# A gated cross-attention and expert layer on one core: loads, casts and the first routing scores are put in another order

## The reference

```
x = x + tanh(g_xattn) * GAT2(GAT1(ctx, adj=layernorm(x)))     # leaky relu, softmax with mask 1e10*(1-adj), elu
n = layernorm(x)
logits = tanh(n @ Wg1.T) @ Wg2.T                              # 8 experts
scores = softmax of the top 2 logits, 0 elsewhere
h = silu(n @ Wup[e].T + bup[e])
x = x + tanh(g_ffn) * sum_e scores[:, e] * (h @ Wdown[e].T + bdown[e])
```

## Time and profile before

| | us |
|---|---|
| median of 3 runs | 97.99 |
| the three runs | 96.74, 97.99, 98.16 |
| the profiled execution's own time | 96.72 |
| its span, first to last instruction | 94.9 |
| between span and time | 1.8 |

### The profile page before, as it was taken

How to read it: one execution, slowest core, us unless ns; L and a number is a source line. 1 busy time by engine, 2 the same in 40 slices (tenths; PEclk the granted TensorE clock), 3 DMA queues, 4 the chain that set the end, 5 groups by cost and what they waited for, 6 DMA issues and landing times.

```text
span 94.9 us, 1971 instructions
## 1 busy us (share of the span) xinstructions
PE 84.5 (89%) x621; PEld 78.9 (83%) x621; DVE 66.9 (70%) x206; ACT 53.4 (56%) x128; POOL 44.4 (47%) x100
## 2 busy tenths in 40 slices
PE   5959999969989689999999999999999999999800
PEld 5936878659878578998999899999999999999700
DVE  5844968374689929999879738977438767889520
ACT  0519785489692761439790979855536555443100
POOL 7910869829018422999780000787100888810000
PEclk9999999999999999999999999999999999999997
DMA  1999990000000000000000000030000030003022
GB/s 26 296 294 410 418 327 6 0 0 0 7 3 0 0 0 0 0 7 3 0 0 3 0 7 0 0 110 3 7 0 0 0 110 0 0 0 116 5 68 67
DMA packets 3339, 5.44 MB, mean 57 GB/s; under 512 B 474, under 2 KB 2684, under 8 KB 3068
## 3 DMA queue, kind: packets, MB, share of 16 engines
q1 hardware_dynamic: 2952, 4.74, 15.0%
q10 hardware_dynamic: 372, 0.53, 1.8%
HBM read 4.21 MB, written 1.05 MB: 55 GB/s over the span
## 4 chain that ended last, share of the span: by engine, by line
PE 52%; DVE 27%; issue 5%; DMA 5%; ACT 4%; POOL 1%; DVEq 1%; ACTq 1%
PE bank L850 6%; PE bank L714 5%; PE bank L759 5%; DMA w_sb<-in_w 5%; PE bank L715 5%; PE bank L719 5%; PE bank L761 5%; PE bank L760 5%; DVE hid_lo L1064 4%; PE bank L874 4%; DVE stat L966 3%; PE bank L734 3%; DVE wdown_hi L1199 2%; DVE xa L1148 2%; DVE hid L1056 2%
## 5 line engine op out<-in xcount | busy, mean ns | idle before, releaser
L504 ACT ACTIVATE act_sb<-bank,small_sb 128x256 f32<-128x256 f32 x32 | 15.1, 472 | 13.7 <-PE bank L719 13.6
L1056 DVE TENSOR_TENSOR hid<-act_sb,bank 128x256 f32<-128x256 f32 x32 | 13.3, 418 | 10.4 <-PE bank L734 8.5
L512 ACT CAST hid_hi<-hid 128x256 fp32r<-128x256 f32 x32 | 13.0, 407 | 11.1 <-DVE hid L1056 10.4
L759 PE MATMUL bank<-wdown_hi,hid_hi 128*128 128x256 f32 x64 | 18.3, 287 | 0.3 <-ACT hid_hi L512 0.3
L714 PE MATMUL bank<-xt_hi,wup_hi 128*128 128x256 f32 x64 | 18.0, 303 | 0.4 <-DVE xa L1148 0.3
L761 PE MATMUL bank<-wdown_hi,hid_lo 128*128 128x256 f32 x64 | 18.0, 281 | 0.0
L760 PE MATMUL bank<-wdown_lo,hid_hi 128*128 128x256 f32 x64 | 18.0, 281 | 0.0
L715 PE MATMUL bank<-xt_hi,wup_lo 128*128 128x256 f32 x64 | 16.5, 280 | 0.0
L1064 DVE TENSOR_TENSOR hid_lo<-hid,hid_hi 128x256 fp32r<-128x256 f32 x32 | 13.5, 422 | 0.3
L714 PEld LDWEIGHTS bank<-xt_hi,wup_hi 128*128 128x128 f32 x64 | 12.1, 189 | 1.0 <-DVE xa L1148 0.5
L719 PE MATMUL bank<-xt_lo,wup_hi 128*128 128x256 f32 x64 | 12.8, 281 | 0.0
(11 more groups left out here) (145 smaller groups left out, 183.5 us busy)
## 6 DMA issues: line engine op xcount, KB each, us to landing
x_sb<-in_x SPq DMA_DIRECT2D x4, 256.0 KB, 4.8
wup_sb<-in_wup SPq DMA_DIRECT2D x1, 1024.0 KB, 7.4
wdown_sb<-in_wdown SPq DMA_DIRECT2D x1, 1024.0 KB, 9.6
out<-out_sb SPq DMA_DIRECT2D x3, 256.0 KB, 2.2
check_sb<-in_check_w SPq DMA_DIRECT2D x1, 320.0 KB
w_sb<-in_w ACTq DMA_DIRECT2D x1, 256.0 KB, 5.0
out<-out_sb SPq DMA_DIRECT2D x2, 128.0 KB, 2.8
ctx_sb<-in_ctx_t ACTq DMA_DIRECT2D x1, 128.0 KB, 4.1
```

The source lines that it names most:

```text
L504: nc.scalar.activation(act_out(n), bank[:, UP[n % 2], 0:N], ACT.Silu, bias=bup_sb[:, k % E:k % E + 1]).then_inc(silu_rdy, 1)
L512: nc.scalar.copy(hid_hi[:, n % HID_SLOTS, :], hid[:, n % 2, :]).then_inc(hid_hi_rdy, 1)
L759: nc.tensor.matmul(dst, hid_hi[:, n % HID_SLOTS, part], wdown_hi[:, e, :], start=False, stop=False, skip_group_check=True)
L1056: nc.vector.tensor_tensor(hid[:, n % 2, :], act_out(n), bank[:, PICK[n % 2], 0:N], ALU.mult).then_inc(hid_rdy, 1)
```

## The change

- Loads. `w0` comes first on SP's queue, then `x` of graph 0, `w1`, `x` of graph 1, the bias row, and the rest as before. ACT's queue carries only the context, now in two pieces: graph 0 and then graphs 1 to 3.
- PE is given 10 products on the constant tile instead of 16. `feat0(2)` stands ahead of `turn(0)`, `feat1(0, 1)` ahead of `twice_part(0)`, and `turn(3)` and `twice_part(3)` move from the loop to the first part. `gather(1)` writes to bank 1 instead of bank 5, so `pe_up` of step 1 waits for `gated(0)` alone, and `pe_pick` of step 0 waits for `gated(1)`. `gather(3)` comes at step 4 instead of 5, the first scores' transpose at step 3 instead of 5.
- DVE. `dve_route` stands right behind `dve_logits`, in seven chained steps instead of nine; `elu1(3)`, `gated(1)` and its statistics come after it. `turned(2)` comes ahead of `dve_norm`, `turned(3)` behind `dve_xt`. `gated` of graphs 1 to 3 is one instruction on 512 elements instead of two on 256. DVE makes `veps` and `nmean` (two small instructions for each graph), which POOL made.
- ACT takes the four `wdown` casts (steps 1, 3, 5, 7), copies `source` of graph 3 at step 0 instead of 4, casts the bias row behind `exp0(0)` instead of first of all, and casts the second quarter of `wup` earlier.
- POOL takes the cast of `pick` (before its one-hots) and both instructions on `bdown`, and makes the one-hots of graph 3 after the first `wup` quarter.

The gathers themselves are the same instructions as before.

PE, the last rows ahead of the loop and its first steps, before. In these listings `x2` and the like count equal instructions in a row.

The diff, cut to its core:

```diff
-WARM_MMS = 16
+WARM_MMS = 10
-SCORE_PLACE = (5, 6, 6, 6)
+SCORE_PLACE = (3, 6, 6, 6)
-        TURN, TWICE, FEAT0, FEAT1, GATHER = (2, 2, 2, 7), (0, 0, 6, 7), (6, 7, 4, 6), (1, 3, 1, 3), ((4, 5), (5, 5), (6, 6), (7, 7))
+        TURN, TWICE, FEAT0, FEAT1, GATHER = (2, 2, 2, 7), (0, 0, 6, 7), (6, 7, 4, 6), (1, 3, 1, 3), ((4, 5), (1, 1), (6, 6), (7, 7))
 # SP
+            sp.dma_start(w0_sb[:], w0).then_inc(w0_ld, 16)
             load_x(0)
+            sp.dma_start(w1_sb[:], w1).then_inc(w1_ld, 16)
             load_x(1)
-            sp.dma_start(ctx_sb[0:FIN, 2 * N:T], ctx_t[:, 2 * N:T]).then_inc(ctx2_ld, 16)
+            sp.wait_ge(bias_zero, 1)
+            sp.dma_start(bias_sb[0:33:32, :], bias_2).then_inc(bias_ld, 16)
 # row_power, POOL
-            pool.wait_ge(mv_rdy, (nb + 1) * C)
-            nc.gpsimd.tensor_scalar(veps[:, pair(b)], mv[:, pair(b), 1], EPS, None, ALU.add).then_inc(veps_rdy, 1)
-            nc.gpsimd.tensor_scalar(nmean[:, pair(b)], mv[:, pair(b), 0], -1.0, None, ALU.mult).then_inc(veps_rdy, 1)
 # POOL
+            pool.wait_ge(pick_raw, 2)
+            nc.gpsimd.tensor_copy(pick[:], pick_f).then_inc(pick_rdy, 1)
+            rows_onehot(1)
+            rows_onehot(2)
             wup_part(0)
             row_power(pool, 0, 0)
+            rows_onehot(3)
             wup_part(1)
             wup_part(2)
+            row_power(pool, 0, 1)
             wup_part(3)
             wdown_part(0)
+            wdown_part(1)
             row_power(pool, 0, 2)
+            nc.gpsimd.tensor_copy(bdown_parts[:], bdown_sb[:]).then_inc(bdown_hi_rdy, 1)
...
 # ACT
-            act.dma_start(ctx_sb[0:FIN, 0:2 * N], ctx_t[:, 0:2 * N]).then_inc(ctx_ld, 16)
-            act.dma_start(w0_sb[:], w0).then_inc(w0_ld, 16)
-            act.dma_start(bias_sb[0:33:32, :], bias_2).then_inc(bias_ld, 16)
-            act.dma_start(w1_sb[:], w1).then_inc(w1_ld, 16)
+            act.dma_start(ctx_sb[0:FIN, 0:N], ctx_t[:, 0:N]).then_inc(ctx_ld, 16)
+            act.dma_start(ctx_sb[0:FIN, N:T], ctx_t[:, N:T]).then_inc(ctx2_ld, 16)
             minus0(0)
             exp0(0)
+            bias_part()
-            act_experts(act, 0, {4: [lambda: source_copy(3)]})
+            act_experts(act, 0, {0: [lambda: source_copy(3)], 1: [lambda: wdown_part(0)],
+                                 3: [lambda: wdown_part(1)], 5: [lambda: wdown_part(2)], 7: [lambda: wdown_part(3)]})
 # PE, pe_up and pe_pick
-                pe.wait_ge(xa_rdy, C * (n + 1))
+                pe.wait_ge(xa_rdy, n + 1)
-            if n < 2:
-                pe.wait_ge(z_rdy, n + 3)
+            if n == 0:
+                pe.wait_ge(xa_rdy, 2 * C)
+            if n == 1:
+                pe.wait_ge(z_rdy, B)
-            pe_experts(pe, 0, {1: [lambda: gather(2), lambda: turn(3)], 3: [lambda: twice_part(3)], 5: [lambda: gather(3)]})
+            pe_experts(pe, 0, {1: [lambda: gather(2)], 4: [lambda: gather(3)]})
 # DVE
             gated(0)
-            stats(0)
+            dve_stats(dve, 0, 0)
+            turned(2)
             dve_norm(dve, 0)
-            turned(2)
...
             dve_logits(dve, 0, 0)
-            gated(1)
-            stats(1)
-            nc.vector.tensor_copy(bdown_parts[:], bdown_sb[:]).then_inc(bdown_hi_rdy, 1)
             dve_route(dve, 0)
             elu1(3)
+            gated(1)
+            dve_stats(dve, 0, 1)
-            dve_experts(dve, 0, {0: [lambda: wdown_part(0)], 1: [lambda: turned(3), lambda: gated(2)],
-                                 2: [lambda: wdown_part(1), lambda: stats(2)], 3: [pick_copy], 4: [bdown_part, lambda: wdown_part(2)],
-                                 6: [lambda: gated(3), lambda: wdown_part(3)], 7: [lambda: stats(3)], 13: [check_peaks],
+            dve_experts(dve, 0, {0: [lambda: gated(2), lambda: dve_stats(dve, 0, 2)],
+                                 5: [lambda: gated(3), lambda: dve_stats(dve, 0, 3)], 13: [check_peaks],
```

More of the change, by code:

```diff
@@ L146, in build @@
         hit = sb("hit", [P, 2, NT, E])
+        same, hit0, prob0 = sb("same", [P, C, 2, E]), sb("hit0", [P, C, 2, E]), sb("prob0", [P, C, 2])
         score = sb("score", [P, NT, E])
@@ L557, in source_copy @@
                 act.wait_ge(twice_mm, b + 1)
-                nc.scalar.copy(source_next[:, b - 1, :, :], both(TWICE[b])).then_inc(source_nextdy, 1)
+                nc.scalar.copy(source_next[:, b - 1, :, :], both(TWICE[b])).then_inc(source_rdy, 1)
             def minus0(b):
@@ L589, in _ @@
             exp1(0)
+            turned(1)
             minus0(3)
             exp0(3)
-            turned(1)
             act.wait_ge(small_ld, 16)
@@ L595, in _ @@
             wup_part(0)
+            wup_part(1)
             source_copy(1)
@@ L599, in _ @@
             exp1(1)
-            wup_part(1)
+            source_copy(2)
             act_xt(act, 0, 0)
@@ L604, in _ @@
             exp1(2)
-            source_copy(2)
             act_gate(act, 0, 0)
@@ L884, in _ @@
             feat0(1)
+            feat0(2)
             turn(0)
-            feat0(2)
             feat1(0, 0)
+            feat1(0, 1)
             twice_part(0)
-            feat1(0, 1)
             feat0(3)
@@ L900, in _ @@
             feat1(2, 1)
+            turn(3)
             feat1(3, 0)
@@ L969, in dve_stats @@
                 nc.vector.bn_aggr(mv[:, t, :], stat[:, t, :]).then_inc(mv_rdy, 1)
+            dve.wait_ge(mv_rdy, C * (run * B + b + 1))
+            nc.vector.tensor_scalar(veps[:, pair(b)], mv[:, pair(b), 1], EPS, None, ALU.add).then_inc(veps_rdy, 1)
+            nc.vector.tensor_scalar(nmean[:, pair(b)], mv[:, pair(b), 0], -1.0, None, ALU.mult).then_inc(veps_rdy, 1)
         def dve_norm(dve, run):
@@ L1145, in gated @@
                     dve.wait_ge(gates_rdy, 1)
+                if b > 0:
+                    dve.wait_ge(gather_mm, C + b)
+                    nc.vector.scalar_tensor_tensor(out=xa[:, pair(b), :], in0=both(GATHER[b][0]), scalar=gates[:, 0:1],
+                                                   in1=x_sb[:, pair(b), :], op0=ALU.mult, op1=ALU.add).then_inc(xa_rdy, C)
+                    return
                 for t in range(C):
-                    dve.wait_ge(gather_mm, t + 1 if b == 0 else C + b)
+                    dve.wait_ge(gather_mm, t + 1)
                     nc.vector.scalar_tensor_tensor(out=xa[:, C * b + t, :], in0=bank[:, GATHER[b][t], t * D:(t + 1) * D],
@@ L1180, in _ @@
             dve_xt(dve, 0, 0)
+            turned(3)
             elu1(2)
```

77 lines of the change are left out of this document (37 added, 40 removed).

## The result

The changed kernel takes **93.27 us** (median of 4 runs, 92.65 to 93.88), the kernel before in the same set of runs 98.07 us (96.74 to 98.78). The ratio is 0.9553 with a 95% interval of 0.943 to 0.9677. The forecast was 93.4 us. The profiled execution took 93.16 us, of which 91.4 us are span; the sum for such an execution was 93.2 us.

The account below looks back on a forecast made before the run. PE bounds from 43 us; from 26.2 to 43 DVE is fuller, earlier engines wait in a chain. 96.72 - 3.3 (three parts) - 0.2 = 93.2, plus 0.2: 93.4 us; own range 92.5 to 94.0, 8 in 10: 92.3 to 95.3.

Parts of the forecast that it names:

- part 1: Head: new load order brings data 2.1 us earlier, graph 0's statistics 0.8 us earlier; bounds -0.1 and -1.3.
- part 2: Norm of graph 0: `veps` and `nmean` on DVE save 0.4 us, `turned(2)` ahead of the power's wait 0.45.
- transposes to step 0: PE works without a gap, 5.8 us plus 0.7 moved from the loop; step 0 starts at 25.3 us.
- rival A: Head gives nothing: data at 4.9 us, bias row late or pace low; 94.0 us, chance 0.20.
- Part 3: Steps 0 to 7: 4.7 us leave DVE, PE's waits of 2.0 us go; 13.0 us become 10.6.
- term of -0.2: Behind step 8: one PE wait, for a silu late under DVE's backlog, goes; -0.2 us.
- rival B: DVE's `veps` and `nmean` of graphs 2 and 3 wait out POOL's `wdown_lo`, delaying `hid`: +1.6, 94.8 us, chance 0.12.
- C: ACT bounds steps 0 to 7, casts standing ahead of silus: full price 2.4 us, 95.6 us, chance 0.08.
- D: Slower than before: PE stays at 1.2 GHz well into the first part; up to 100.7 us, chance 0.04.
- E: New load order holds up graph 1's `x` or `wup`: +1 to 2 us, 94.4 to 95.4, chance 0.04.
- 0.2 us for the spread: Added to the sum because work begins at 4.0 us, so a late rise of PE's pace costs at least as much.
- rule on shared interfaces: GpSimd and VectorE share SBUF interfaces, so more POOL work means more DVE collisions; counted against the change, no separate size.

Follow-up runs that it names:

- old loads: Changed kernel with the old load order and queues, 16 constant products and early bias cast: 94.44 us, ratio 0.9724.
- order alone: Changed kernel's PE, ACT, DVE and POOL order, shorter scores' chain and one-instruction `gated`, with loads, norm and casts of the kernel before: 98.87 us, six runs in two groups.
- repetition: Changed kernel run again, nothing altered but a blank line: 93.32 us, ratio 0.9625.
- old norm: Changed kernel with `veps` and `nmean` on POOL for all graphs and `turned(2)` behind the wait for the power: 94.45 us, ratio 0.9773.
- old casts: Changed kernel with the `wdown`, `pick` and `bdown` casts back on DVE, in the new order: 96.12 us, ratio 0.984.
- casts alone: Kernel before with only the `wdown` casts moved to ACT and `pick` and `bdown` to POOL: 97.22 us, ratio 1.0035.
- `nmean` on POOL: Changed kernel with `veps` and `nmean` of graphs 1 to 3 back on POOL, graph 0's on DVE: 93.8 us, ratio 0.969.
- context in halves: Changed kernel with the context loaded as graphs 0 and 1, then 2 and 3, both on ACT's queue: 94.23 us, ratio 0.9716.

## Why the prediction was right, step by step

Every mark came within 0.4 us of its forecast, but some of it got there by another way than I gave.

| step | forecast | measured |
|---|---|---|
| part 1, at the statistics | -0.8 | -0.69 |
| part 2, statistics to transposes | -0.85 | -0.67 |
| transposes to step 0 | 6.6 | 6.59 |
| steps 0 to 7 | 10.6 | 10.18 |
| step 8 begins | 35.9 | 35.77 |
| a wait behind step 8 goes | -0.2 | 0 |
| profiled execution | 93.2 | 93.16 |

**Part 1, right in size, one term missing.** The arithmetic from the first product to `elu0(0)` held in its sum: 2.1 - 0.9 - 0.3 was forecast and 2.16 - 0.75 - 0.67 measured. PE's low pace cost twice what I took, and the bias a little less. What did not hold is "keep it that size up to the statistics of graph 0". I had costed the reordering at nothing, and it gives 0.27 us: in nine profiles of kernels with the new order in the first part, whatever their loads, the end of `elu0(0)` lies 7.09 or 7.10 us ahead of the statistics (8.98 and 16.07 with the old loads, 9.46 and 16.55 in the order alone), in the kernel before 7.36 (9.23 and 16.59). The first profile of the changed kernel is an exception with 7.41; its second context piece landed at 6.9 us, in the repetition at 6.2. That swallowed in this execution what the order gives, and it is luck that -0.69 is so near to -0.8.

What the loads give is known less well. With the new order and no late rise of PE's pace the statistics come at 15.61 to 15.94 with the new loads and ten or sixteen constant products (seven profiles), and at 16.07 and 16.55 with the old ones (two profiles), where `w0` landed at 5.83 and at 6.31 us; in the kernel before it landed at 6.08. So the loads are worth 0.1 to 0.9 us, by when they happen to land. My 0.8 lies inside, and rival A, that they give nothing, is neither shown nor ruled out.

**Part 2, right.** Both terms are in the old norm's rows, with 0.67 us together instead of 0.85. What is missing lies in a wait that the doubled product used to cover: PE now stands still for 0.39 us until ACT's `xn` is there, at 19.00.

**Part 3, right in sum, wrong about who pays.** I wrote that the casts, 4.7 us of DVE's time, made it late in steps 0 to 7, and that moving them ends PE's waits there. The order alone takes those waits away with the casts still on DVE (10.11 us for the eight steps), and so does the new order in the old casts' kernel (10.12). The casts alone leave all three waits and shorten one, by 0.56 us. With the new order, what they are worth shows only at steps 10 and 11: with the casts on DVE the first `hid` comes at 41.0 to 41.6 and PE waits 1.3 to 1.7 us for it. In the kernel before this backlog was hidden, because PE was itself late. So the parts don't add: in the profiles the casts alone give 1.0 us in the loop and the order alone 0.1 (after taking off the 0.7 that is moved), both together 2.15, or 2.5 with `nmean` out of the way. By the times neither is shown to be worth anything alone. I counted one wait as removed without asking how late DVE would then be at the next place.

**The term of -0.2, and rival B.** This term failed. The wait that I meant, for a silu at step 11, was to go with DVE's backlog. It is still there: the weight load that waits for `act_sb` stands idle for 0.30 us, against 0.39 before. Its old cause did go (the casts alone have no such wait), but B came true in its mechanism: `nmean` of graph 3 waited out POOL's `wdown_lo`, 1.26 us for what took 0.16 us at 16.97, and held up `hid` and the silu behind it. I had priced B at up to 1.6 us; most of it fell into slack, since `hid` still came 2.5 us after step 8 as before, and PE lost 0.36 us, as the kernel with `nmean` on POOL shows. So the old cause and the new one cost the same: step 8 to the last product up took 40.00 us before and 39.99 now.

**Rivals C, D and E.** ACT has 4.0 us of the window to spare and delays PE once, by the 0.30 us at 39.50, which comes from the late `hid`. The loads held up nothing behind the head. D did not happen as priced; a small form of it, a late rise, is in the spread, and the one run of 143.13 us with a single constant product shows that a clock of 0.58 over a whole run occurs. With ten or sixteen it was in none of the runs.

**The 0.2 us for the spread, and the range.** Most kernels' runs lie 1.2 to 3.6 us apart. In most profiled executions the later `feat0` products are at the fast pace, and in three not one of the first twelve or eight is (old casts, context in halves, casts alone); those three start the statistics 1.1 to 1.4 us later than the kernels that they are compared with, and then lose nothing more by it. With one constant product the first eight were slow as well, but the pace rose at 7.80 us, where in those three it rose behind 9 us, and the statistics were not late. The loss of 1.1 to 1.4 us is as much as most of the differences between the medians of this study. The Trainium skill says in "TensorE: Matmul & The Clock Gate", section "Part 1: The HAM clock gate", that how many products run at the low clock differs from run to run of one kernel. The traces go with it as far as two like heads can show it: the same loads and constant products give eight products in 1.99 us before and in 3.75 with the casts alone. No kernel was profiled in both ways. My own range, 92.5 to 94.0, is not what the bounds of part 1 give: -0.1 and -1.3 instead of -0.8 make it 92.9 to 94.1. And E's 94.4 to 95.4 is counted from the forecast, where A to C are counted from the sum of 93.2.

**The rule on shared interfaces.** The collisions found here were with one input of 128x2 (1.26 and 1.25 us), one input of 128x512 (1.07 against 0.42) and two inputs of 16x256 (1.06 against 0.41). The Trainium skill's "GPSIMD Engine Reference", section "Key points", names two inputs or a two-port mode; the `bdown` row fits the first of these, and whether the others are in such a mode no run here shows. In the prediction I said that two-input `hid_lo` was not hit; in the kernel with the casts on DVE one took 0.83 us (at 41.92, under POOL's 1.27 at 41.20) and in the order alone another (at 42.51), so that held for the kernel before and not in general.
